# Feed-forward expert sum as one chain of adds on GpSimd, gated products written in place into an eight-slot ring

## Chip, cores and metric

One core of a Trainium2 chip runs the whole program. The metric is the device time of one execution in microseconds (us). Five engines work at the same time and wait for each other through semaphores: TensorE (PE in the profile), VectorE (DVE), ScalarE (ACT), GpSimd (POOL), and SyncE (SP), which issues the transfers.

## What is computed

The reference is a layer of three parts on 4 x 512 tokens of width 256: half a mixture-of-experts feed-forward, attention, and the same half feed-forward again with the same weights. The change touches only the feed-forward, which runs twice:

```python
def _L0_ffn_ref(x, router_w, router_b, expert_w, expert_b, proj_w, proj_b, norm_w):
    B, S, D = x.shape                      # 4, 512, 256
    E = router_b.shape[0]                  # 8
    logits = jnp.einsum('bsd,de->bse', x, router_w) + router_b
    topk_vals, topk_idx = jax.lax.top_k(logits, TOP_K)     # 2
    topk_w = jax.nn.softmax(topk_vals, axis=-1)
    full_w = jnp.sum(jax.nn.one_hot(topk_idx, E, dtype=x.dtype) * topk_w[..., None], axis=-2)
    h = jnp.einsum('td,edf->etf', xf, expert_w) + expert_b[:, None, :]
    expert_out = jax.nn.silu(h)
    combined = jnp.einsum('etf,te->tf', expert_out, full_w.reshape(-1, E)).reshape(B, S, D)
    out = jnp.einsum('bsd,df->bsf', combined, proj_w) + proj_b
    y = x + out
    rms = jnp.sqrt(jnp.mean(y * y, axis=-1, keepdims=True) + EPS)
    return norm_w * (y / rms)
...
x = x + 0.5 * _L0_ffn_ref(_layernorm(x, axis=-1), ...)
```

All eight experts are computed for every token; a token's weight is zero for six of them. `combined` is the sum that the change rebuilds.

## The kernel before

`ffn_phase` is called twice, first with the prefix f1 (the first some 170 us of the span) and then with f2 (the last some 150 us); attention lies between. Each phase takes the tokens in four batches of 512 (`SEQ`). Batch 0 is written out, batches 1 and 2 are a hardware loop (`Fori(1, LAST)`), batch 3 is written out with `more=False`. Every engine has its own program, in which `body(i, prev, more)` is batch `i`; nothing is scheduled by a planner, and the order on an engine is the order in which its code is written. The profile drops the prefix and the buffer number, so that f_s is `s_ring` of either phase.

Within a batch the features lie on the 128 partitions in two halves (`C = 2`, index `f`) and the tokens along the free axis, so that one tile is 128x512 in float32. For each expert `e` and half `f`, with `n = 2e + f`:

- TensorE forms the expert's product in bank `ex_ps[n % 4]` with six matmuls (L749 to L751), and spreads the token's weight for expert `e` over the partitions with one matmul into `w_ps[e % 2]` (`select`, L762).
- ScalarE applies silu into `s_ring[n % 4]` (L603). It waits for `mult_done`, so that the slot's previous product has been read.
- VectorE multiplies the slot by the weight in `w_ps` (L482). The product of expert 0 goes to `acc`, the others to `u_ring[n % 4]`.
- The sum: GpSimd adds the products of experts 1, 2 and 3 to `acc` (L293). VectorE adds product 4 to product 5, and 6 to 7, as pairs in `u_ring` (L506, two instructions of 128x512 a pair), and GpSimd adds each pair to `acc` by two more L293. That makes 10 adds on GpSimd and 4 on VectorE a batch. Between expert 3 and the pairs, GpSimd's program has `residual` (L256, z plus the projection's bias) and `add_rows` (L275, the previous batch's result added to x; not in batch 0).

What follows the sum of batch `i` runs inside batch `i + 1`. ScalarE rounds `acc` to `ch` (`sum_lead`, L610), VectorE takes the remainder `cl` (`sum_rest`, L403), TensorE projects them into `w_ps` (`project`, L771 to L773, 24 matmuls), VectorE adds the residual (L436), ScalarE squares (L620), VectorE forms the mean square (L441), GpSimd its inverse root (`inverse_rms`, L270), and VectorE scales the rows (`scale_rows`, L446). `acc` is free for batch `i + 1` once `cl` is there.

VectorE's `gating` of batch `i + 1` (L364 to L393) comes right after the last product and pair of batch `i`, and before `sum_rest(i)`. It is a chain of some twenty small instructions that ends in `fw`. TensorE transposes `fw` (`weights_T`, L735) and then runs `project(i)`; both stand in its program behind experts 0, 1 and 2 of batch `i + 1`. The inputs of some of these small instructions all lie in SBUF (the gap of the two best logits L372, the cast of the indices L376, the one-hot rows and what is made of them L379 to L393); the first two (L364, L367) have one input in PSUM, as L482 has.

In phase f1 alone, ScalarE and VectorE also split the attention weights into two parts (L628, L452; 128x1280), and GpSimd scales them (L265).

Batch 3 sums otherwise: GpSimd adds products 1 and 2 to `acc`, then forms 3 + 4 + 5 in place (L303, L308), and VectorE forms 6 + 7 and adds both (L409, L416).

Of the kernel before, what the change touches and what calls it, by code (L numbers as in the profile page):

```python
# [15 lines left out]
F32 = mybir.dt.float32  # L16
# [40 lines left out]
def ffn_phase(nc, tag, d, shared, step_sems, passed, first, split, out):  # L57
# [16 lines left out]
    with ExitStack() as ctx:  # L74
# [41 lines left out]
        fw = sb("fw", [P, BT, P])  # L116
        wT = sb("wT", [P, SEQ], F32R)

        s_ring = [sb(f"s{n}", [P, SEQ]) for n in range(4)]
        u_ring = [sb(f"u{n}", [P, SEQ]) for n in range(4)]  # L120
        acc = sb("acc", [P, C, SEQ])
        ch, cl = sb("ch", [P, C, SEQ], F32R), sb("cl", [P, C, SEQ], F32R)

# [1 line left out]
        pick_raw = sq[0:2 * E].rearrange("p t d -> p (t d)").rearrange("p (e q) -> p e q", e=E)  # L125


        last5 = sq[:].rearrange("p (c t) d -> p c (t d)", c=C)
        ch_last, cl_last = e_hi[:, 0:C, :], e_lo[:, 0:C, :]
        ss, ms, rr = sb("ss", [P, BT]), sb("ms", [P, BT]), sb("rr", [P, BT])  # L130
        if first:
# [25 lines left out]
        step_ps = t_ps + w_ps + w_ps  # L157
        RING = len(ex_ps)
        SILU0 = RING
        MULT0 = len(s_ring)  # L160
        X0 = 1


        SUMS = (1, 2, 3, 5, 7)
        ACC = C * len(SUMS)
        PAIRS = C * 2
        GATE = 20
        LAST = BATCH - 1

# [71 lines left out]
        def _(pool):  # L241
# [35 lines left out]
            def body(i, prev, more):  # L277
                if more or first:
                    rstd(i + 1)
                if prev:  # L280
                    inverse_rms(i - 1)
                if first:
                    scale_queries(i)
                for j, e in enumerate(SUMS if more else SUMS[:2]):
                    for f in range(C):
                        n = C * e + f
                        if e < 4:
                            pool.wait_ge(mult_done, MULT0 + C * E * i + n + 1)
                        else:
                            pool.wait_ge(pair_done, PAIRS * i + C * (e // 2 - 2) + f + 1)  # L290
                        if j > 0:
                            pool.wait_ge(acc_done, ACC * i + C * (j - 1) + f + 1)
                        pool.tensor_tensor(acc[:, f, :], acc[:, f, :], u_ring[n % 4][:], ALU.add).then_inc(acc_done, 1)  # L293
                    if e == 3:
                        residual(i + 1)
                        if prev:
                            add_rows(i - 1)
                if not more:

                    for f in range(C):  # L300
                        e3, e4 = (u_ring[(C * e + f) % 4] for e in (3, 4))
                        pool.wait_ge(mult_done, MULT0 + C * E * i + C * 4 + f + 1)
                        pool.tensor_tensor(e4[:], e4[:], e3[:], ALU.add).then_inc(acc_done, 1)  # L303
                    for f in range(C):
                        e4 = u_ring[(C * 4 + f) % 4]
                        pool.wait_ge(mult_done, MULT0 + C * E * i + C * 5 + f + 1)
                        pool.wait_ge(acc_done, ACC * i + C * 2 + f + 1)
                        pool.tensor_tensor(e4[:], e4[:], last5[:, f, :], ALU.add).then_inc(acc_done, 1)  # L308
                    add_rows(i - 1)

            if first:
# [12 lines left out]

        @block.vector
        def _(dve):
            dve.sem_inc(mult_done, MULT0)

            def norm_stats(j):
                b, k = block_of(j), (j - J0) * BT  # L330
                if isinstance(j, int) and j >= BATCH:
# [72 lines left out]

            def add_sixth(f):

                e6, e7 = s_ring[(C * 6 + f) % 4], s_ring[(C * 7 + f) % 4]
                dve.wait_ge(mult_done, MULT0 + C * E * LAST + C * 7 + f + 1)
                dve.tensor_tensor(e7[:], e7[:], e6[:], ALU.add).then_inc(pair_done, 1)  # L409

            def add_middle(f):

                e7 = s_ring[(C * 7 + f) % 4]
                dve.wait_ge(pair_done, PAIRS * LAST + 2 * f + 1)
                dve.wait_ge(acc_done, ACC * LAST + C * 3 + f + 1)
                dve.tensor_tensor(e7[:], e7[:], u_ring[(C * 4 + f) % 4][:], ALU.add).then_inc(pair_done, 1)  # L416

            def last_rest():
                for f in range(C):
                    dve.wait_ge(chi_done, C * BATCH + f + 1)  # L420
                    dve.tensor_tensor(cl_last[:, f, :], s_ring[(C * 7 + f) % 4][:], ch_last[:, f, :].bitcast(F32),
                                      ALU.subtract).then_inc(clo_done, 1)

            def add_last_residual(t):
# [29 lines left out]
            def body(i, prev, more):  # L454
                if not prev:
                    norm_stats(i + 1)
                gating(i)
                if prev:
                    sum_rest(i - 1)
                    if more or first:  # L460
                        norm_stats(i + 1)
                    add_residual(i - 1, 0)
                    add_residual(i - 1, 1)
                else:
                    norm_rows(i + 1)
                    expert_rest(4)
                    expert_rest(5)
                group_at = (3, 6) if more else (2, 3)
                for e in range(E):
                    for f in range(C):  # L470
                        n = C * e + f
                        dve.wait_ge(silu_done, SILU0 + C * E * i + n + 1)
                        if f == 0:
                            dve.wait_ge(sel_done, E * i + e + 1)
                        if e in (3, 4) or more and e in (5, 7):
                            dve.wait_ge(acc_done, ACC * i + C * (3 if e == 7 else e - 3) + f + 1)
                        if more and e == 6:
                            dve.wait_ge(pair_done, PAIRS * i + f + 1)
                        to = acc[:, f, :] if e == 0 else u_ring[n % 4][:]
                        if not more and e >= 5:  # L480
                            to = last5[:, f, :] if e == 5 else s_ring[n % 4][:]
                        dve.tensor_tensor(to, s_ring[n % 4][:], w_ps[e % 2][:], ALU.mult).then_inc(mult_done, 1)  # L482
                        if not more and e == E - 1:
                            if f > 0:
                                add_middle(f - 1)
                            add_sixth(f)
                    if e == 0 and prev:
                        mean_square(i - 1)
                    if e == 0 and prev and (more or first):
                        norm_rows(i + 1)  # L490
                    if e == 0 and not prev:
                        expert_rest(6)
                        expert_rest(7)
                        dve.wait_ge(e_hi_done, E + 1)
                        dve.tensor_tensor(p_lo[:], p_raw, p_hi[:].bitcast(F32), ALU.subtract).then_inc(p_split, 1)
                    if e == 2 and prev:
                        scale_rows(i - 1)
                    if e == 4 and (more or first):
                        z_rest(i + 1)
                    if e == 4 and not more:  # L500
                        sum_rest(i)
                    if more and e in (5, 7):
                        dve.wait_ge(mult_done, MULT0 + C * E * i + C * e + C)
                        for f in range(C):
                            even, odd = u_ring[(C * (e - 1) + f) % 4], u_ring[(C * e + f) % 4]
                            dve.tensor_tensor(odd[:], odd[:], even[:], ALU.add).then_inc(pair_done, 1)  # L506
                    if first and e in group_at:
                        group_rest(i, group_at.index(e))
                if not more:
                    add_middle(C - 1)  # L510
# [62 lines left out]
        def _(act):  # L573
# [24 lines left out]
            def silu(i, e, chunks=range(C)):  # L598
                for f in chunks:
                    n = C * e + f  # L600
                    act.wait_ge(ex_done, C * E * i + n + 1)
                    act.wait_ge(mult_done, C * E * i + n + 1)
                    act.activation(s_ring[n % 4][:], ex_ps[n % RING][:], ACT.Silu,  # L603
                                   bias=e_bias[:, n:n + 1]).then_inc(silu_done, 1)

            def sum_lead(i):
# [4 lines left out]

            def last_lead():
                for f in range(C):
                    act.wait_ge(pair_done, PAIRS * LAST + 2 * f + 2)
                    act.activation(ch_last[:, f, :], s_ring[(C * 7 + f) % 4][:], ACT.Copy).then_inc(chi_done, 1)

            def squares(i):
                for t in range(BT):
# [79 lines left out]
        def _(pe):  # L698
# [55 lines left out]
            def select(i, e, prev):  # L754
# [3 lines left out]
                if e < 2 and prev:  # L758
                    pe.wait_ge(yadd_done, 2 * (i - 1) + e + 1)
                if e >= 2:  # L760
                    pe.wait_ge(mult_done, MULT0 + C * E * i + C * (e - 1))
                pe.matmul(w_ps[e % 2][:], pick[:, e, :], wT[:], start=True, stop=True).then_inc(sel_done, 1)  # L762

            def project(i):
# [34 lines left out]
            def step_project(k):  # L799

                if k == 2:
                    pe.wait_ge(mult_done, MULT0 + C * E * BATCH)
# [837 lines left out]
```

## Time and profile before

| | us |
|---|---|
| median of three runs | 892.91 (891.31 to 893.33) |
| the profiled execution | 892.65 |
| its span, from the first to the last instruction | 890.8 |
| busy: PE, DVE, POOL, ACT | 822.6, 701.0, 585.2, 521.4 |
| mean granted TensorE clock | 0.971 of full |

The span is a little shorter than the time of the same execution; what lies around it is 1.85 us. The busy times are over the whole span, and attention, which the change doesn't touch, takes some 570 us of it. A matmul's busy time overlaps with the next one's, so that PE's share reads higher than its work.

### The profile page before, as it was taken

To read this page: it belongs to the slowest core of one execution; us is meant where nothing else is said; L and a number is where in the kernel's file an instruction comes from. 1 tells how busy PE (TensorE), PEld (TensorE's weight loads), DVE (VectorE), ACT (ScalarE), POOL (GpSimd) and SP (SyncE) were. 2 spreads that over 40 slices of the span, in tenths; PEclk is the share of its full clock that TensorE was granted. 3 is DMA by queue.
4 is the path that set the end of the run, shared out by engine and by line. 5 is a ranking of instruction groups with operands and counts; after the bars stand their busy time and mean duration, and the time that the engine had idled before them with its cause. 6 is when DMAs were issued, how large, how long until landed. Compare 5 with 4: busy or idle time off the path is not lost. (4 is left out here: it accounts for less than half of the span.)

```text
span 890.8 us, 17017 instructions
## 1 busy us (share of the span) xinstructions
PE 822.6 (92%) x4848; PEld 724.0 (81%) x4848; DVE 701.0 (79%) x1824; ACT 521.4 (59%) x1252; POOL 585.2 (66%) x444
## 2 busy tenths in 40 slices
PE   5998888767999999999999999999999998999984
PEld 4776776656889999999999899899999986787873
DVE  6899989899776776776866867767767797789987
ACT  3654534445765765755865766756767663554542
POOL 3667746368587687777777787777777812556743
PEclk9999988978999999999999999999999999899998
DMA  8053153410212311312312312212212100000001
GB/s 302 1 178 105 72 201 142 142 36 12 49 24 59 106 24 35 94 35 59 94 24 47 94 24 71 85 33 47 71 41 54 25 1 29 1 1 24 24 1 47
DMA packets 26673, 55.98 MB, mean 63 GB/s; under 512 B 3568, under 2 KB 9840, under 8 KB 25104
## 3 DMA queue, kind: packets, MB, share of 16 engines
q1 hardware_dynamic: 26640, 55.59, 21.4%
q8 instruction: 15, 0.25, 0.1%
q14 instruction: 18, 0.15, 0.1%
HBM read 22.02 MB, written 12.58 MB: 39 GB/s over the span
## 5 line engine op out<-in xcount | busy, mean ns | idle before, releaser
L1050 POOL TENSOR_TENSOR at_ql<-at_rot,at_qh 128x512 fp32r<-128x512 f32 x62 | 79.8, 1287 | 99.6 <-ACT at_qh L1272 99.6
L1289 ACT ACTIVATE at_pr<-at_sm,at_low 128x512 f32<-128x512 f32 (+3 forms) x256 | 140.4, 555 | 0.9 <-DVE at_low L1137 0.8
L1295 ACT ACTIVATE at_pth<-at_pt 128x512 fp32r<-128x512 f32 (+1 forms) x192 | 95.8, 525 | 76.0 <-PE at_pt L1449 75.2
L603 ACT ACTIVATE f_s<-f_ex,f_cols 128x512 f32<-128x512 f32 x128 | 84.1, 686 | 86.0 <-PE f_ex L751 46.3
L293 POOL TENSOR_TENSOR f_acc<-f_acc,f_u 128x512 f32<-128x512 f32 x68 | 100.8, 1509 | 40.8 <-DVE f_u L482 27.7
L1147 DVE TENSOR_SCALAR at_pr<-at_pr,at_inv 128x128 f32<-128x128 f32 (+3 forms) x256 | 113.1, 504 | 2.3
L1137 DVE CUSTOM_DVE_ANT_0 at_sm<-at_sc,at_mask 128x512 f32<-128x512 f32 (+3 forms) x256 | 109.8, 484 | 2.5 <-issue 2.4
L1152 DVE TENSOR_TENSOR at_ptl<-at_pt,at_pth 128x512 fp32r<-128x512 f32 (+1 forms) x192 | 108.7, 593 | 1.7 <-ACT at_pth L1295 1.5
L1059 POOL TENSOR_TENSOR at_rot<-ga,cos 128x512 f32<-128x512 f32 x78 | 104.2, 1336 | 4.1 <-POOL at_ql L1050 2.4
L1065 POOL TENSOR_TENSOR at_rot<-at_rot,gc 128x512 f32<-128x512 f32 x78 | 101.5, 1301 | 8.1 <-POOLq L1082 2.1
L1449 PE MATMUL at_pt<-ident,at_pr 128*128 128x128 f32 x640 | 96.3, 278 | 9.3 <-DVE at_pr L1147 6.8
L1061 POOL TENSOR_TENSOR gc<-gc,sin 128x512 f32<-128x512 f32 x78 | 102.2, 1311 | 0.0
L749 PE MATMUL f_ex<-zh,f_e_hi 128*128 128x512 f32 (+1 forms) x240 | 97.5, 406 | 0.0
L750 PE MATMUL f_ex<-zl,f_e_hi 128*128 128x512 f32 (+1 forms) x240 | 96.8, 403 | 0.0
L751 PE MATMUL f_ex<-zh,f_e_lo 128*128 128x512 f32 (+1 forms) x240 | 96.3, 401 | 0.0
L1272 ACT ACTIVATE at_qh<-at_rot 128x512 fp32r<-128x512 f32 x64 | 40.4, 631 | 92.8 <-POOL at_rot L1065 90.7
L1436 PE MATMUL at_sc<-at_kh,at_qh 128*128 (+4 forms) x256 | 89.4, 349 | 3.9 <-DVE at_ql L1228 3.9
L1449 PEld LDWEIGHTS at_pt<-ident,at_pr 128*128 128x128 f32 x640 | 73.2, 142 | 15.4 <-DVE at_pr L1147 7.6
L1437 PE MATMUL at_sc<-at_kl,at_qh 128*128 (+4 forms) x256 | 84.1, 328 | 0.0
L1438 PE MATMUL at_sc<-at_kh,at_ql 128*128 (+4 forms) x256 | 83.7, 327 | 0.0
L1463 PE MATMUL at_o<-at_pth,at_vh 128*128 128x512 f32 (+3 forms) x256 | 82.7, 323 | 0.0
L1465 PE MATMUL at_o<-at_pth,at_vl 128*128 128x512 f32 (+3 forms) x256 | 82.5, 322 | 0.0
(212 smaller groups left out, 2262.7 us busy)
## 6 DMA issues: line engine op xcount, KB each, us to landing
gc<-ga SPq DMA_DIRECT2D x160, 128.0 KB, 2.3
ga<-in_attn_w SPq DMA_DIRECT2D x4, 1280.0 KB, 7.7
attn_split<-gb SPq DMA_DIRECT2D x4, 1280.0 KB, 9.6
attn_split<-gc SPq DMA_DIRECT2D x4, 1280.0 KB, 12.1
gb<-attn_split SPq DMA_DIRECT2D x8, 512.0 KB, 4.2
at_wo<-attn_split SPq DMA_DIRECT2D x8, 512.0 KB, 4.3
x<-in_x SPq DMA_DIRECT2D x4, 512.0 KB, 9.0
e_raw<-in_expert_w SPq DMA_DIRECT2D x8, 256.0 KB, 6.7
```

Source lines behind the costliest of these rows:

```text
L293: pool.tensor_tensor(acc[:, f, :], acc[:, f, :], u_ring[n % 4][:], ALU.add).then_inc(acc_done, 1)
L749: pe.matmul(bank, hi[:, w], zh[:, c, b], start=(c == 0), stop=False)
L750: pe.matmul(bank, hi[:, w], zl[:, c, b], start=False, stop=False)
L751: r = pe.matmul(bank, lo[:, w], zh[:, c, b], start=False, stop=(c == C - 1))
L1059: pool.tensor_tensor(rot[r % 2][:], raw[r], cosT[:], ALU.mult)
L1061: pool.tensor_tensor(swap[r], swap[r], sinT[:], ALU.mult).then_inc(sin_done, 1)
L1065: pool.tensor_tensor(rot[r % 2][:], rot[r % 2][:], swap[r], ALU.add).then_inc(sum_done, 1)
L1137: dve.tensor_tensor_reduce(out=sm[h % 2][:, OFF[i]:OFF[i] + w], in0=sc[bank][:, col:col + w], in1=mask[:, SEQ - w:SEQ], scale=1.0, scalar= ...
L1147: dve.tensor_scalar(a, a, inv[h % 2][:, i:i + 1], None, ALU.mult).then_inc(nm_done, 1)
L1152: dve.tensor_tensor(ptl[h % 2][:, cols], pt[(NF * h + k) % 2][:, 0:FLEN[k]], pth[h % 2][:, cols].bitcast(F32), ALU.subtract).then_inc(lo_d ...
L1289: act.activation(pr[h % 2][:, cols], sm[h % 2][:, cols], ACT.Exp, bias=low[h % 2][:, i:i + 1], scale=-1.0, accum_out=tot[h % 2][:, i:i + 1 ...
L1449: r = pe.transpose(pt[(NF * h + k) % 2][:, col + (i - kt) * P:col + (i - kt + 1) * P], pr[h % 2][:, OFF[i] + kt * P:OFF[i] + (kt + 1) * P] ...
```

## The change

The pair adds on VectorE are gone. GpSimd adds the products of experts 1 to 7 to `acc` one after the other, 14 adds a batch in batches 0 to 2. `u_ring` is gone, and `s_ring` has eight slots in its place: VectorE writes the product over the silu that it was made from, and GpSimd reads it there. So a slot is free for the silu four experts later only when GpSimd has added it (for expert 4, when VectorE has made product 0, which goes to `acc` and leaves the slot unused). In batch 3 the places of some products change, the number of adds and their engines don't.

```diff
-        s_ring = [sb(f"s{n}", [P, SEQ]) for n in range(4)]
-        u_ring = [sb(f"u{n}", [P, SEQ]) for n in range(4)]
+        s_ring = [sb(f"s{n}", [P, SEQ]) for n in range(8)]
...
-        SUMS = (1, 2, 3, 5, 7)
+        SUMS = range(1, E)
...
                 for j, e in enumerate(SUMS if more else SUMS[:2]):
                     for f in range(C):
                         n = C * e + f
-                        if e < 4:
-                            pool.wait_ge(mult_done, MULT0 + C * E * i + n + 1)
-                        else:
-                            pool.wait_ge(pair_done, PAIRS * i + C * (e // 2 - 2) + f + 1)
+                        pool.wait_ge(mult_done, C * E * i + n + 1)
                         if j > 0:
                             pool.wait_ge(acc_done, ACC * i + C * (j - 1) + f + 1)
-                        pool.tensor_tensor(acc[:, f, :], acc[:, f, :], u_ring[n % 4][:], ALU.add).then_inc(acc_done, 1)
+                        pool.tensor_tensor(acc[:, f, :], acc[:, f, :], s_ring[n % SLOTS][:], ALU.add).then_inc(acc_done, 1)
                     if e == 3:
                         residual(i + 1)
                         if prev:
...
                         dve.wait_ge(silu_done, SILU0 + C * E * i + n + 1)
                         if f == 0:
                             dve.wait_ge(sel_done, E * i + e + 1)
-                        if e in (3, 4) or more and e in (5, 7):
-                            dve.wait_ge(acc_done, ACC * i + C * (3 if e == 7 else e - 3) + f + 1)
-                        if more and e == 6:
-                            dve.wait_ge(pair_done, PAIRS * i + f + 1)
-                        to = acc[:, f, :] if e == 0 else u_ring[n % 4][:]
-                        if not more and e >= 5:
-                            to = last5[:, f, :] if e == 5 else s_ring[n % 4][:]
-                        dve.tensor_tensor(to, s_ring[n % 4][:], w_ps[e % 2][:], ALU.mult).then_inc(mult_done, 1)
+                        slot = s_ring[n % SLOTS][:]
+                        to = acc[:, f, :] if e == 0 else slot
+                        dve.tensor_tensor(to, slot, w_ps[e % 2][:], ALU.mult).then_inc(mult_done, 1)
...
-                    if more and e in (5, 7):
-                        dve.wait_ge(mult_done, MULT0 + C * E * i + C * e + C)
-                        for f in range(C):
-                            even, odd = u_ring[(C * (e - 1) + f) % 4], u_ring[(C * e + f) % 4]
-                            dve.tensor_tensor(odd[:], odd[:], even[:], ALU.add).then_inc(pair_done, 1)
...
                     act.wait_ge(ex_done, C * E * i + n + 1)
-                    act.wait_ge(mult_done, C * E * i + n + 1)
-                    act.activation(s_ring[n % 4][:], ex_ps[n % RING][:], ACT.Silu,
+                    if e == 4:
+                        act.wait_ge(mult_done, C * E * i + f + 1)
+                    elif e > 4:
+                        act.wait_ge(acc_done, ACC * i + C * (e - 5) + f + 1)
+                    elif not (isinstance(i, int) and i == 0):
+                        act.wait_ge(acc_done, ACC * (i - 1) + C * (e + 3) + f + 1)
+                    act.activation(s_ring[n % SLOTS][:], ex_ps[n % RING][:], ACT.Silu,
                                    bias=e_bias[:, n:n + 1]).then_inc(silu_done, 1)
```

GpSimd's program at the end of batch 0 of phase f1, from the residual on; before:

```order
L256 TENSOR_TENSOR f1_zres<-z,f1_rows 128x1024
L293 TENSOR_TENSOR f1_acc<-f1_acc,f1_u2 128x512
L293 TENSOR_TENSOR f1_acc<-f1_acc,f1_u3 128x512
L293 TENSOR_TENSOR f1_acc<-f1_acc,f1_u2 128x512
L293 TENSOR_TENSOR f1_acc<-f1_acc,f1_u3 128x512
```

The same place now (the changed kernel's lines are numbered anew, L287 is the add to `acc`):

```order
L253 TENSOR_TENSOR f1_zres<-z,f1_rows 128x1024
L287 TENSOR_TENSOR f1_acc<-f1_acc,f1_s0 128x512
L287 TENSOR_TENSOR f1_acc<-f1_acc,f1_s1 128x512
L287 TENSOR_TENSOR f1_acc<-f1_acc,f1_s2 128x512
L287 TENSOR_TENSOR f1_acc<-f1_acc,f1_s3 128x512
L287 TENSOR_TENSOR f1_acc<-f1_acc,f1_s4 128x512
L287 TENSOR_TENSOR f1_acc<-f1_acc,f1_s5 128x512
L287 TENSOR_TENSOR f1_acc<-f1_acc,f1_s6 128x512
L287 TENSOR_TENSOR f1_acc<-f1_acc,f1_s7 128x512
```

Four adds behind the residual have become eight; in batches 1 and 2 `add_rows` stands between the residual and them, before and now.

VectorE's program at the same place, from the products of expert 5 to the cast in the gating; before:

```order
L482 TENSOR_TENSOR f1_u2<-f1_s2,f1_wide1 128x512
L482 TENSOR_TENSOR f1_u3<-f1_s3,f1_wide1 128x512
L506 TENSOR_TENSOR f1_u2<-f1_u2,f1_u0 128x512
L506 TENSOR_TENSOR f1_u3<-f1_u3,f1_u1 128x512
L482 TENSOR_TENSOR f1_u0<-f1_s0,f1_wide0 128x512
L482 TENSOR_TENSOR f1_u1<-f1_s1,f1_wide0 128x512
L452 TENSOR_TENSOR gc<-ga,gb 128x1280
L482 TENSOR_TENSOR f1_u2<-f1_s2,f1_wide1 128x512
L482 TENSOR_TENSOR f1_u3<-f1_s3,f1_wide1 128x512
L506 TENSOR_TENSOR f1_u2<-f1_u2,f1_u0 128x512
L506 TENSOR_TENSOR f1_u3<-f1_u3,f1_u1 128x512
```

And now (L469 is the product, L444 the split of the attention weights):

```order
L469 TENSOR_TENSOR f1_s2<-f1_s2,f1_wide1 128x512
L469 TENSOR_TENSOR f1_s3<-f1_s3,f1_wide1 128x512
L469 TENSOR_TENSOR f1_s4<-f1_s4,f1_wide0 128x512
L469 TENSOR_TENSOR f1_s5<-f1_s5,f1_wide0 128x512
L444 TENSOR_TENSOR gc<-ga,gb 128x1280
L469 TENSOR_TENSOR f1_s6<-f1_s6,f1_wide1 128x512
L469 TENSOR_TENSOR f1_s7<-f1_s7,f1_wide1 128x512
```

The four pair adds have left VectorE, and what followed each pair stands right behind the products; the gating is next in both.

## Rows read from the trace of the kernel before

**Rows 1.** Busy time by stretch: stretch, us, busy (instructions) by engine, granted clock, DMA.

```profile
50.00:80.00 30.00, 26.52 (x126) 21.59 (x125) 29.05 (x53) 15.57 (x29) 21.11 (x15) 0.94 0.24 97
...
819.00:851.00 32.00, 29.76 (x148) 24.64 (x148) 30.26 (x72) 15.68 (x31) 21.22 (x14) 1.00 0.05 17
```

**Rows 2.** Timeline of TensorE, ends of batches: start, us, what [idle before, releaser].

```profile
52.08 0.66 PE L735 MATMUL f_t<-ident,f_fw 128*128 128x128 f32 x4 [0.33 <-DVE f_fw L393]
...
87.79 0.66 PE L735 MATMUL f_t<-ident,f_fw 128*128 128x128 f32 x4 [1.15 <-DVE f_fw L393]
...
123.34 1.11 PE L735 MATMUL f_t<-ident,f_fw 128*128 128x128 f32 x4 [2.55 <-DVE f_fw L393]
...
787.50 0.60 PE L735 MATMUL f_t<-ident,f_fw 128*128 128x128 f32 x4
...
819.09 0.66 PE L735 MATMUL f_t<-ident,f_fw 128*128 128x128 f32 x4 [1.60 <-DVE f_fw L393]
820.29 0.39 PE L771 MATMUL f_wide<-f_p_hi,f_ch 128*128 128x256 f32 x1 [0.55 <-DVE f_cl L403]
```

**Rows 3.** Timeline of GpSimd, phase f2, batch 1.

```profile
795.47 5.41 POOL L293 TENSOR_TENSOR f_acc<-f_acc,f_u 128x512 f32<-128x512 f32 x4 [0.65 <-DVE f_u L482]
...
807.19 2.84 POOL L275 TENSOR_TENSOR x<-x,f_y 128x1024 f32 x1
810.00 3.00 POOL L293 TENSOR_TENSOR f_acc<-f_acc,f_u 128x512 f32<-128x512 f32 x2
814.60 2.83 POOL L293 TENSOR_TENSOR f_acc<-f_acc,f_u 128x512 f32<-128x512 f32 x2 [1.61 <-DVE f_u L506]
```

**Rows 4.** Timeline of VectorE, phase f2, batch 1 and the gating behind it.

```profile
797.10 4.45 DVE L446 SCALAR_TENSOR_TENSOR f_y<-f_y,f_rr,f_rows 128x256 f32<-128x256 f32 x4
...
806.37 4.21 DVE L506 TENSOR_TENSOR f_u<-f_u 128x512 f32<-128x512 f32 x2
...
814.96 0.18 DVE L364 TENSOR_TENSOR f_l<-f_t,f_rows 128x32 f32<-128x32 f32 x1
...
815.93 0.28 DVE L372 TENSOR_TENSOR f_gap<-f_top 128x4 f32<-128x4 f32 x1
...
816.81 0.66 DVE L376 CAST f_topf<-f_topi 128x8 f32<-128x8 uint32 x1
...
818.09 0.18 DVE L386 TENSOR_TENSOR f_oh<-f_oh,f_w 128x32 f32<-128x32 f32 x1
```

**Rows 5.** Timeline of GpSimd, phase f1, batches 0 and 1.

```profile
38.59 2.42 POOL L256 TENSOR_TENSOR f_zres<-z,f_rows 128x1024 f32<-128x1024 f32 x1
...
47.51 2.92 POOL L293 TENSOR_TENSOR f_acc<-f_acc,f_u 128x512 f32<-128x512 f32 x2 [1.60 <-DVE f_u L506]
...
74.40 2.39 POOL L275 TENSOR_TENSOR x<-x,f_y 128x1024 f32 x1
...
83.30 2.84 POOL L293 TENSOR_TENSOR f_acc<-f_acc,f_u 128x512 f32<-128x512 f32 x2 [1.60 <-DVE f_u L506]
```

**Rows 6.** Timeline of VectorE, phase f1, the second split in batch 1.

```profile
79.06 1.48 DVE L452 TENSOR_TENSOR gc<-ga,gb 128x1280 fp32r<-128x1280 f32 x1
```

**Rows 7.** The adds on GpSimd by their line: count, ns min/median/max.

```profile
L293 POOL TENSOR_TENSOR f_acc<-f_acc,f_u x68: 1263/1315/2637, 29.8 to 863.3; 128x512 f32<-128x512 f32 x68
```

**Rows 8.** Timeline of GpSimd and VectorE, phase f2, batch 0.

```profile
765.71 7.56 POOL L293 TENSOR_TENSOR f_acc<-f_acc,f_u 128x512 f32<-128x512 f32 x6 [10.92 <-DVE f_u L482]
...
781.61 2.92 POOL L293 TENSOR_TENSOR f_acc<-f_acc,f_u 128x512 f32<-128x512 f32 x2 [1.60 <-DVE f_u L506]
...
785.78 0.17 DVE L382 TENSOR_SCALAR f_w<-f_th 128x4 f32<-128x4 f32 x1 [0.89 <-ACT f_th L587]
```

**Rows 9.** Busy time by stretch: the 24 matmuls of a projection, twice.

```profile
88.90:91.80 2.90, 2.81 (x24) 2.81 (x25) 2.59 (x11) 0.20 (x2) 0.74 (x1) 1.00 0.98 413
124.50:129.80 5.30, 5.25 (x24) 5.25 (x25) 2.55 (x10) 1.50 (x5) 1.02 (x1) 0.50 1.00 409
```

**Rows 10.** Timeline of VectorE, phase f1, batch 3.

```profile
150.50 1.87 DVE L482 TENSOR_TENSOR f_s<-f_s,f_wide 128x512 f32<-128x512 f32 x3
```

More of the change, by code:

```diff
@@ L125, in ffn_phase @@
         pick_raw = sq[0:2 * E].rearrange("p t d -> p (t d)").rearrange("p (e q) -> p e q", e=E)
-        last5 = sq[:].rearrange("p (c t) d -> p c (t d)", c=C)
         ch_last, cl_last = e_hi[:, 0:C, :], e_lo[:, 0:C, :]
@@ L159, in ffn_phase @@
         SILU0 = RING
-        MULT0 = len(s_ring)
+        SLOTS = len(s_ring)
         X0 = 1
-        SUMS = (1, 2, 3, 5, 7)
+        SUMS = range(1, E)
         ACC = C * len(SUMS)
-        PAIRS = C * 2
         GATE = 20
@@ L300, in body @@
                     for f in range(C):
-                        e3, e4 = (u_ring[(C * e + f) % 4] for e in (3, 4))
-                        pool.wait_ge(mult_done, MULT0 + C * E * i + C * 4 + f + 1)
+                        e3, e4 = (s_ring[(C * e + f) % SLOTS] for e in (3, 4))
+                        pool.wait_ge(mult_done, C * E * i + C * 4 + f + 1)
                         pool.tensor_tensor(e4[:], e4[:], e3[:], ALU.add).then_inc(acc_done, 1)
                     for f in range(C):
-                        e4 = u_ring[(C * 4 + f) % 4]
-                        pool.wait_ge(mult_done, MULT0 + C * E * i + C * 5 + f + 1)
+                        e4, e5 = (s_ring[(C * e + f) % SLOTS] for e in (4, 5))
+                        pool.wait_ge(mult_done, C * E * i + C * 5 + f + 1)
                         pool.wait_ge(acc_done, ACC * i + C * 2 + f + 1)
-                        pool.tensor_tensor(e4[:], e4[:], last5[:, f, :], ALU.add).then_inc(acc_done, 1)
+                        pool.tensor_tensor(e4[:], e4[:], e5[:], ALU.add).then_inc(acc_done, 1)
                     add_rows(i - 1)
@@ L326, in _ @@
         def _(dve):
-            dve.sem_inc(mult_done, MULT0)
             def norm_stats(j):
@@ L405, in add_sixth @@
             def add_sixth(f):
-                e6, e7 = s_ring[(C * 6 + f) % 4], s_ring[(C * 7 + f) % 4]
-                dve.wait_ge(mult_done, MULT0 + C * E * LAST + C * 7 + f + 1)
+                e6, e7 = (s_ring[(C * e + f) % SLOTS] for e in (6, 7))
+                dve.wait_ge(mult_done, C * E * LAST + C * 7 + f + 1)
                 dve.tensor_tensor(e7[:], e7[:], e6[:], ALU.add).then_inc(pair_done, 1)
             def add_middle(f):
-                e7 = s_ring[(C * 7 + f) % 4]
-                dve.wait_ge(pair_done, PAIRS * LAST + 2 * f + 1)
+                e4, e7 = (s_ring[(C * e + f) % SLOTS] for e in (4, 7))
+                dve.wait_ge(pair_done, 2 * f + 1)
                 dve.wait_ge(acc_done, ACC * LAST + C * 3 + f + 1)
-                dve.tensor_tensor(e7[:], e7[:], u_ring[(C * 4 + f) % 4][:], ALU.add).then_inc(pair_done, 1)
+                dve.tensor_tensor(e7[:], e7[:], e4[:], ALU.add).then_inc(pair_done, 1)
             def last_rest():
@@ L420, in last_rest @@
                     dve.wait_ge(chi_done, C * BATCH + f + 1)
-                    dve.tensor_tensor(cl_last[:, f, :], s_ring[(C * 7 + f) % 4][:], ch_last[:, f, :].bitcast(F32),
+                    dve.tensor_tensor(cl_last[:, f, :], s_ring[(C * 7 + f) % SLOTS][:], ch_last[:, f, :].bitcast(F32),
                                       ALU.subtract).then_inc(clo_done, 1)
@@ L613, in last_lead @@
                 for f in range(C):
-                    act.wait_ge(pair_done, PAIRS * LAST + 2 * f + 2)
-                    act.activation(ch_last[:, f, :], s_ring[(C * 7 + f) % 4][:], ACT.Copy).then_inc(chi_done, 1)
+                    act.wait_ge(pair_done, 2 * f + 2)
+                    act.activation(ch_last[:, f, :], s_ring[(C * 7 + f) % SLOTS][:], ACT.Copy).then_inc(chi_done, 1)
             def squares(i):
@@ L760, in select @@
                 if e >= 2:
-                    pe.wait_ge(mult_done, MULT0 + C * E * i + C * (e - 1))
+                    pe.wait_ge(mult_done, C * E * i + C * (e - 1))
                 pe.matmul(w_ps[e % 2][:], pick[:, e, :], wT[:], start=True, stop=True).then_inc(sel_done, 1)
@@ L801, in step_project @@
                 if k == 2:
-                    pe.wait_ge(mult_done, MULT0 + C * E * BATCH)
+                    pe.wait_ge(mult_done, C * E * BATCH)
                 if k >= 4:
```

## Prediction

> **What bounds the kernel now.** I read the page first, then the busy time by stretch, then TensorE's timeline at the ends of the batches, and last GpSimd's and VectorE's beside each other. The page's totals mix three phases, so the stretches matter more: VectorE is busy for 29.05 of 30 us in the loop of f1 and 30.26 of 32 in that of f2, TensorE for 26.5 and 29.8, GpSimd for 21.1 and 21.2 [rows 1]. That reads like a case for taking work from VectorE. But a share doesn't say who ends last. TensorE waits at one place in each batch of both phases: before `weights_T`, for `fw`, and once more, by 0.55 us, before `project`, for `cl` [rows 2]. In f2 it starts `weights_T` at 819.09 after 1.60 idle and `project` at 820.29. So what a batch costs is set by when the gating chain and the last add to `acc` are done, and GpSimd has a hand in both. The last add of f2's batch 1 ends at 814.60 + 2.83 = 817.43 [rows 3]; the gating's cast, begun at 816.81, takes 0.66 and ends with it [rows 4], while the same chain's other small instructions take 0.2 to 0.3. It stands still while GpSimd adds.
>
> The second thing to see is how the two engines alternate. `scale_rows` is four instructions of 256 columns with both inputs in SBUF. Beside four adds on GpSimd they take 4.45 us together, 1.1 each [rows 4], and the adds 5.41, 1.35 each [rows 3]: one of VectorE, one of GpSimd, in turn. With nothing in SBUF against them, six adds take 7.56, 1.26 each [rows 8], and none of the 68 took under 1.263 [rows 7].
>
> **The change, part by part.** *GpSimd's tail.* After `add_rows` (in batch 0 after `residual`) there are now eight adds in place of four. Everything up to there depends on `project` of the batch before and not on the pairs, so it starts where it did. In f2's batch 1 `add_rows` starts at 807.19. It took 2.84 beside VectorE's pair, 2.39 without one in f1 [rows 3, 5], and the pair is gone: the adds start at 809.6. By then the products are there: the rest of VectorE's list before the gating is six products, free of the 4.21 us that the pair took [rows 4]. I count three adds at 1.26 until the gating asks for its first SBUF pair, and five at 1.35 in turn with it: 10.5 us, the end at 820.1 in place of 817.43, **2.7 later**. The bounds are 8 x 1.26 = 10.1 and 8 x 1.35 = 10.8, that is 2.3 to 3.0. In f1's batch 1, `add_rows` ends at 74.40 + 2.39 = 76.8 [rows 5], and the second split (1.48 [rows 6]) gets its turn among the adds: 76.8 + 10.5 + 1.5 = 88.8 in place of 83.30 + 2.84 = 86.14, **2.7 later**; batch 2 is the same. In f1's batch 0 the residual ends at 38.59 + 2.42 = 41.0, and the adds at 53.0 in place of 50.43 [rows 5], **2.6 later**. In f2's batch 0 the residual ends at 765.71 + 7.56 + 2.42 = 775.7 [rows 5, 8], the adds at 786.2 in place of 784.53 [rows 8], **1.7 later**.
>
> *The gating.* VectorE reaches it earlier, by the pairs; in f2 it then waits for TensorE's logits, in f1 it can start some 1.3 us sooner. That helps nothing if it must take turns: from the gap on, at least eight of its instructions have all inputs in SBUF (the gap, the cast, two one-hot rows, two weightings, their sum, the remainder in `fw`), while five or fewer adds are left. Each add lets one of them through, so the chain ends only behind the last add, with what is then left of it. Before, the chain from the second weighting (818.09) to TensorE's start (819.09) took 1.0 [rows 2, 4]; I take 1.0 + 0.1 behind the last add. `weights_T` would start at 821.2 in f2 (+2.1), 89.9 in f1's batch 1 (from 87.79, +2.1), 125.5 in its batch 2 (from 123.34, +2.1), 54.1 in its batch 0 (from 52.08, +2.0). `project` keeps its 1.2 us behind it. In f2's batch 0 the gating waits for ScalarE's tanh at 785.78 already [rows 8], and `weights_T` had no wait at 787.50 [rows 2]; I take +0.6. Bounds for each place: +1.2, if the chain slips through between adds (then only `cl` waits for the last add: 2.7 less the 1.5 by which `project` at 820.29 trails the last add beyond the two 0.6 us steps of `ch` and `cl`), and +3.0. Six places: 2.0 + 2.1 + 2.1 + 0.6 + 2.1 + 2.1 = **11.0 us**.
>
> On this row and rule differ in what they count. The Trainium skill, page "SBUF — State Buffer", section "Who interferes with whom", has the lock on the shared ports as exclusive for the whole instruction, and lists scalar-operand instructions, copies and casts among those that can take it. By that page the two weights L382 and L383 would wait for a turn too, an estimate of 0.3 us more at each of five places, 1.5 in all. The same page says that issue order decides who blocks; it doesn't say that the two alternate, which [rows 3, 4] show.
>
> *TensorE's clock.* In f1 its wait of 1.15 us before `weights_T` of batch 1 was followed by a projection at granted clock 1.00 in 2.90 us, the wait of 2.55 in batch 2 by one at 0.50 in 5.30 us [rows 2, 9]. So a halved clock costs 2.4 there, at once, since GpSimd's whole list hangs on the projection. The waits become 1.15 + 2.1 = 3.3, 1.60 + 2.1 = 3.7 in f2 twice, and 0.33 + 2.0 = 2.3 in f1's batch 0; f1's batch 2 pays already, and f2's batch 0 has no such wait. Three places for certain enough, one at even chance: 2.4 x 3.5 = **8.4 us**. Bounds: none, or 2.4 at four places, 9.6.
>
> *Costed at nothing.* The pair adds leave VectorE (4 a batch, 4.21 for the costlier two of f2 [rows 4]): TensorE is what waits, and it waits behind GpSimd. If that cover were gone, this would be the gain of the rival below. The product in place: same inputs, one in PSUM, same length. The new waits of silu on `acc_done`: behind silu of expert 4 to 7 stand adds of experts 1 to 3, done long before; behind those of the next batch's experts 0 and 1 stand the adds of 4 and 5, of which the last ends at about 83.3 in f1 and 815 in f2, level with TensorE's own product. What queues behind a late one is the tanh on ScalarE and then the two weights, which wait for GpSimd's turn anyway; priced from 0 to 0.3. Batch 3: its silu of expert 7 is released sooner, but VectorE runs expert 6 and 7 in one piece from 150.50 for 1.87 [rows 10], so nothing comes of it.
>
> **Sum.** 11.0 + 8.4 = 19.4 on the profiled execution's own 892.65 (span 890.8) gives 912.0. That execution is within 0.3 of the median of the runs, 892.91, so the prediction is **912 us**, 2.1% slower.
>
> **Rivals.**
>
> 1. *GpSimd is late, but the gating slips through.* If VectorE gets more than one small instruction done between two adds, `weights_T` starts nearly on time and only `project` waits: 5 x 1.2 + 0.3 = 6.3, and TensorE's wait is cut in two, so that the clock halves at perhaps one place more: 899 to 903, say 901. For it: the small instructions take under 0.2. Against it: `scale_rows`, four in a row without a dependence, took strict turns.
>
> 2. *Faster.* VectorE is what ends last, and losing the pairs lets the gating start sooner. TensorE's waits of 0.33, 1.15 and 2.55 in f1 and 1.60 twice in f2 could go [rows 2], at most 7.2 with the 0.55 left, and with one halved clock (2.4) 9.6: 883 to 887. It decides at the length of an add: the eight must end by 817.43 from 809.6, so each within 0.98 us. None of the 68 was under 1.263 [rows 7]. Only if the gating held the ports first and the adds weren't what `cl` waits for could this win.
>
> 3. *No change.* The lateness is hidden behind the 1.5 us of slack at `cl`, and the gating's earlier start pays for its turns: 893. It needs adds that end at most 1.5 later; I work out 2.7, at least 2.3.
>
> 4. *Slower still.* The halved clock reaches into the expert products behind the projection and into silu's waits, 1.5 to 2 more at each of five places: 920 to 923.
>
> **How the numbers follow.** The main case has 0.62, with its own range 905 to 918 (places at +1.6 to +2.6, two to four halved clocks). Rival 1 has 0.18, rival 2 0.07, rival 3 0.05, rival 4 0.08. A measurement of this kernel can tell some 0.2%, 1.8 us, from no change. Slower is 0.62 + 0.18 + 0.08 = 0.88, same 0.05, faster 0.07. The range leaves out rivals 2, 3, 4 and reaches into rival 1 to 899; at the top 919.
>
> **What the changed profile would show.** Eight adds in a row on GpSimd behind `add_rows`, 10 to 11 us in f2 and 12 in f1, with GpSimd idle only before `rstd`; the gap, cast and one-hot instructions of the gating at 1.2 to 1.4 us apart in place of 0.2; `weights_T` 3.3 to 3.7 us idle for `fw`; granted clock 0.5 in most projections; VectorE's busy time down by about 20 us and its waits up; a loop period of f2 of some 36 us in place of 32. It would be wrong if the chain of the gating ends before GpSimd's last add (rival 1), if the projections keep clock 1.00 after waits over 3 us (8 us less), or if adds run shorter than 1.26.

## The result, and the profile after

The changed kernel takes 904.24 us (median of four, 903.23 to 906.58) against 892.11 in the runs beside it: ratio 1.0146, interval 1.0129 to 1.0163, slower by some 12 us. Each experiment below has its ratio to runs of the kernel before made beside it, whose medians lie between 891.33 and 891.79; a difference between two other kernels is that of their medians, and is good to about 1 us. The profiled executions have spans of 901.4 and 890.8, so the profile has 10.6 of it.

TensorE's timeline at the ends of the batches, changed kernel, against [rows 2]:

```profile
53.27 0.66 PE L722 MATMUL f_t<-ident,f_fw 128*128 128x128 f32 x4 [1.81 <-DVE f_fw L385]
...
91.72 1.12 PE L722 MATMUL f_t<-ident,f_fw 128*128 128x128 f32 x4 [2.45 <-DVE f_fw L385]
...
129.70 1.12 PE L722 MATMUL f_t<-ident,f_fw 128*128 128x128 f32 x4 [3.92 <-DVE f_fw L385]
...
825.39 1.08 PE L722 MATMUL f_t<-ident,f_fw 128*128 128x128 f32 x4 [3.20 <-DVE f_fw L385]
```

The waits of 0.33, 1.15, 2.55 and 1.60 us are now 1.81, 2.45, 3.92 and 3.20, and the fifth, behind f2's batch 2, is 3.28 in place of 1.65. GpSimd's timeline, phase f2, batch 1, against [rows 3]:

```profile
809.55 2.41 POOL L253 TENSOR_TENSOR f_zres<-z,f_rows 128x1024 f32 x1
811.91 2.40 POOL L272 TENSOR_TENSOR x<-x,f_y 128x1024 f32 x1
814.26 9.97 POOL L287 TENSOR_TENSOR f_acc<-f_acc,f_s 128x512 f32<-128x512 f32 x8
```

Eight adds run without a hole, 1.25 us each, right behind `add_rows`. VectorE's gating beside them, against [rows 4]:

```profile
816.76 0.19 DVE L356 TENSOR_TENSOR f_l<-f_t,f_rows 128x32 f32<-128x32 f32 x1 [2.80 <-PE f_t L716]
...
817.74 0.33 DVE L364 TENSOR_TENSOR f_gap<-f_top 128x4 f32<-128x4 f32 x1
818.66 0.66 DVE L368 CAST f_topf<-f_topi 128x8 f32<-128x8 uint32 x1
819.36 1.24 DVE L371 TENSOR_TENSOR f_oh<-f_rows,f_topf 128x32 f32<-128x32 f32 x1
820.51 1.32 DVE L372 TENSOR_TENSOR f_oh<-f_rows,f_topf 128x32 f32<-128x32 f32 x1
821.76 1.28 DVE L374 TENSOR_SCALAR f_w<-f_th 128x4 f32<-128x4 f32 x1
822.96 1.30 DVE L375 TENSOR_SCALAR f_w<-f_th 128x4 f32<-128x4 f32 x1
824.29 0.19 DVE L377 TENSOR_TENSOR f_oh<-f_oh,f_w 128x32 f32<-128x32 f32 x1
...
825.16 0.18 DVE L385 TENSOR_TENSOR f_fw<-f_full,f_full_hi 128x32 f32<-128x32 f32 x1
825.26 1.28 DVE L395 TENSOR_TENSOR f_cl<-f_acc,f_ch 128x512 fp32r<-128x512 f32 x2
```

Four instructions of 32 or 4 columns (L371 to L375) take 1.24 to 1.32: one for each add. In the kernel before, where the last add ended at 817.43, the same ones took 0.2 and less:

```profile
817.50 0.19 DVE L379 TENSOR_TENSOR f_oh<-f_rows,f_topf 128x32 f32<-128x32 f32 x1
...
817.72 0.16 DVE L382 TENSOR_SCALAR f_w<-f_th 128x4 f32<-128x4 f32 x1
```

The last add ends at 824.23, and the next instruction (L377) is back at 0.19. VectorE waited 2.80 us for TensorE's logits before all this: its head start was worth nothing there.

The projections' stretches in the changed kernel (stretch, us, busy by engine, granted clock), to be read with [rows 9]; each ends with its last residual add:

```profile
54.47:59.00 4.53, 4.53 (x26) 4.49 (x27) 2.51 (x10) 0.70 (x4) 1.02 (x1) 0.67 0.29 122
92.90:97.20 4.30, 4.28 (x26) 4.24 (x27) 2.61 (x11) 1.24 (x4) 1.02 (x1) 0.75 0.05 19
130.90:136.30 5.40, 5.40 (x25) 5.39 (x26) 2.50 (x11) 1.46 (x5) 1.02 (x1) 0.53 0.36 133
793.10:796.30 3.20, 3.20 (x26) 3.16 (x27) 2.54 (x11) 0.57 (x4) 1.02 (x1) 1.00 0.00 0
826.60:830.80 4.20, 4.20 (x26) 4.16 (x27) 2.50 (x10) 1.02 (x4) 1.02 (x1) 0.73 0.00 0
861.20:866.60 5.40, 5.40 (x25) 5.40 (x26) 0.69 (x1) 1.42 (x5) 0.00 (x0) 0.52 0.00 0
```

Five of the six meet a halved clock for part or all of their time (a mean between 0.5 and 1 is a stretch that is part at 1.2 and part at 2.4 GHz). Only the one after f2's batch 0, with no wait ahead of `weights_T`, is at 1.00. The length of the wait alone doesn't say how much of a projection is halved: behind 3.20 us it took 4.22, behind 3.28 it took 5.48, and in the kernel before 3.16 behind 1.60 us.

### The profile page after: what moved, and what is told of

Its sections match the earlier page's. It is cut to its first block and busy times, and to the rows that moved or that the text cites. A ratio compares the mean times of both kernels' runs of the same rounds, so it can differ in the third digit from the quotient of the medians.

```text
span 901.4 us, 16986 instructions
## 1 busy us (share of the span) xinstructions
PE 828.0 (92%) x4848; PEld 729.1 (81%) x4848; DVE 698.5 (77%) x1800; ACT 521.6 (58%) x1252; POOL 609.4 (68%) x468
## 3 DMA queue, kind: packets, MB, share of 16 engines
q1 hardware_dynamic: 26640, 55.59, 21.2%
## 5 line engine op out<-in xcount | busy, mean ns | idle before, releaser
L287 POOL TENSOR_TENSOR f_acc<-f_acc,f_s 128x512 f32<-128x512 f32 x92 | 125.8, 1400 | 26.2 <-DVE f_s L469 26.2
```

The source lines that it names most:

```text
L287: pool.tensor_tensor(acc[:, f, :], acc[:, f, :], s_ring[n % SLOTS][:], ALU.add).then_inc(acc_done, 1)
```

## Where the 10.6 us of the profile are

I cut each phase at two events, the start of `project` and the last residual add behind it, in both traces; batch 0 of each phase counts from the phase's first `weights_T`.

| part | f1 b0 | f1 b1 | f1 b2 | f2 b0 | f2 b1 | f2 b2 | sum |
|---|---|---|---|---|---|---|---|
| up to `project`: adds and gating | 1.50 | 1.43 | 1.39 | -1.35 | 1.59 | 1.56 | 6.1 |
| the projection: clock | 1.31 | 1.03 | -0.08 | 0.00 | 1.06 | 2.44 | 5.8 |

For f2's batch 1, for example, the last residual add before it starts at 791.53 and `project` at 820.29 before (28.76), 796.25 and 826.60 after (30.35). The rest, -1.3, is 0.3 ahead of the first `weights_T`, 0.2 in attention (neither traced) and 0.8 behind the last projection. That last one is a loss of 0.4 in batch 3, where VectorE now waits 1.57 us for the silu of expert 7, and a gain of 1.2 in the last 11 us, where the granted clock is 0.69 before and 0.80 after. The -1.35 is by the clock too: it lies behind f2's wait for the first `fw` (3.1 us in both kernels); there the granted clock of the next 8 us is 0.57 before and 0.78 after:

```profile
757.10:765.00 7.90, 7.11 (x20) 5.51 (x21) 5.51 (x12) 3.44 (x6) 0.00 (x0) 0.57 0.00 0
```

```profile
763.20:771.00 7.80, 7.02 (x26) 5.60 (x27) 6.92 (x14) 4.69 (x8) 0.73 (x1) 0.78 0.00 0
```

Adds and gating cost 7.5 us at five places. The other 3 are mostly clock: 5.8 lost in the projections, 1.35 and 1.2 gained elsewhere.

## The experiments

**The ring alone.** The change has two parts. This run has the eight slots and the product in place, and the pairs back on VectorE:

```diff
-        SUMS = range(1, E)
+        PAIRED = (5, 7)
+        SUMS = [e for e in range(1, E) if e + 1 not in PAIRED]
...
+                    if more and e in PAIRED:
+                        dve.wait_ge(mult_done, C * E * i + C * e + C)
+                        for f in range(C):
+                            even, odd = s_ring[(C * (e - 1) + f) % SLOTS], s_ring[(C * e + f) % SLOTS]
+                            dve.tensor_tensor(odd[:], odd[:], even[:], ALU.add).then_inc(pair_done, 1)
```

> The eight-slot ring and the product in place alone; the pair adds stay on VectorE (10 adds a batch on GpSimd, 4 on VectorE, as before). Theory (the cost is GpSimd's chain of eight adds behind add_rows, and the gating taking turns with it): 892 us, within 2 of before, adds ending where they did. Rival (silu now waits for GpSimd's adds through the ring, and that costs): 898 to 904, with ScalarE waiting for acc.

886.27 us, ratio 0.9926 (0.9906 to 0.9945). Neither was right: the ring costs nothing, and it gains 6. Taken in this order, the ring first and the chain on top of it, the change is a gain of 6 and a loss of some 18 in one. VectorE's products of experts 6 and 7, f2, batch 1, in this run:

```profile
806.69 2.47 DVE L474 TENSOR_TENSOR f_s<-f_s,f_wide 128x512 f32<-128x512 f32 x4
809.20 1.29 DVE L498 TENSOR_TENSOR f_s<-f_s 128x512 f32<-128x512 f32 x2
```

Four products in one piece, the pair right behind. In the kernel before, the last product of expert 7 waited for GpSimd to have added the pair that lay in its slot.

**The ring with VectorE's old waits for GpSimd put back,** those of experts 3, 4, 5 and 7. In the kernel before, as in this run, VectorE stood idle for one of them only, once a batch, for 3.5 us in all.

```diff
+                        if e in (3, 4) or more and e in (5, 7):
+                            dve.wait_ge(acc_done, ACC * i + C * (3 if e == 7 else e - 3) + f + 1)
                         slot = s_ring[n % SLOTS][:]
```

> The ring with the pairs kept (886.3), and VectorE's old waits for acc_done ahead of the products of experts 3, 4, 5 and 7 put back; nothing else. Theory (the ring's 6 us come from the product of expert 7 no longer waiting 0.6 us for GpSimd at each batch's end): the wait of 0.5 to 0.7 is back in each of six batches, the last adds end where they did before: 890 to 893. Rival (they come from silu no longer waiting for the product four earlier): 886.

891.98 us, ratio 0.9999 (0.9988 to 1.0011). The 6 us are gone, all of them, and the rival with them:

```profile
808.83 1.95 DVE L476 TENSOR_TENSOR f_s<-f_s,f_wide 128x512 f32<-128x512 f32 x3
811.34 0.69 DVE L476 TENSOR_TENSOR f_s<-f_s,f_wide 128x512 f32<-128x512 f32 x1 [0.56 <-POOL f_acc L292]
812.92 2.85 POOL L292 TENSOR_TENSOR f_acc<-f_acc,f_s 128x512 f32<-128x512 f32 x2 [1.61 <-DVE f_s L500]
```

The wait totals 3.5 us in six places. From `project` to the last add of f2's batch 1 it is 29.10 us here and 28.33 without it. The other 2 to 3 us are not traced one by one; TensorE's waits before `weights_T` are shorter in the ring alone (0.87 in f2's batch 1, 1.61 here), with fewer halved clocks behind them (mean clock 0.976 and 0.969).

**Half the chain.** Only the pair 6 + 7 on VectorE (`PAIRED = (7,)`), 12 adds on GpSimd.

> The changed kernel with the pair 6 + 7 back on VectorE: 12 adds a batch on GpSimd, 2 on VectorE. Theory: the tail behind add_rows is six adds in place of eight, 2.5 us shorter, and about two of the gating's turns go with it; at each of five places between 0 and 0.8 us late in place of 1.2 to 1.6, hardly a halved clock: 893 to 898, say 895. Rival (only that VectorE's pairs are gone matters, by VectorE reaching the gating early): half way, 898.

892.49 us, ratio 1.0006 (0.9987 to 1.0024), just under the range expected. Two adds more on GpSimd than the ring alone cost 6, four cost 18. Six adds behind `add_rows` take 8.42 us, with the pair among them.

**The gating without its turns.** The cast, the weights, the weighted row and the sum go into free columns of the logits' PSUM bank, so that nearly every instruction of the chain has at most one input in SBUF. GpSimd's program is untouched. Done to the changed kernel and to the kernel before:

```diff
                 lp = t_ps[1][:].rearrange("p (t k) -> p t k", t=BT)
+                topf, half0, full = lp[:, :, 16:18], lp[:, :, 24:32], lp[:, :, 40:48]
+                w0, w1 = lp[:, :, 48:49], lp[:, :, 49:50]
...
-                dve.tensor_tensor(oh0[:], oh0[:], w0[:].unsqueeze(2).to_broadcast([P, BT, E]), ALU.mult).then_inc(gate, 1)
+                dve.tensor_tensor(half0, oh0[:], w0.to_broadcast([P, BT, E]), ALU.mult).then_inc(gate, 1)
```

> The changed kernel with the gating's small tiles (index, weights, weighted row, sum) in free columns of the PSUM bank of the logits, so that of its instructions only the gap and the copy into fw have all operands in SBUF. GpSimd's adds stay as they are. Theory (the gating is late because its instructions take turns with the adds): cast, one-hot rows and weights at under 0.3 us each in place of 1.2 to 1.3, weights_T without a wait for fw in f2, project 1.4 us behind the last add in place of 2.4, some waits now short enough to keep the clock: 895 to 899, say 897. Rival (only the last add's end matters, the gating's delay is hidden): 904.

> The kernel before with the gating's small tiles in PSUM. Theory (the turns cost the kernel before too, at the cast): project 2.3 behind the last add in place of 2.85 at five places, so 0.5 each, and one more if a halved clock goes: 887 to 890, say 889. Rival: no change.

Changed kernel 898.97 us, ratio to before 1.0079 (1.0061 to 1.0097), 5 less than without the edit. Kernel before 887.79, ratio 0.9949 (0.9931 to 0.9968): the turns cost it too, and `project` follows the last add of f2's batch 1 by 2.34 us in place of 2.86. VectorE and TensorE of the first, f2, batch 1:

```profile
816.77 0.17 DVE L376 TENSOR_SCALAR f_t<-f_th 128x4 f32<-128x4 f32 x1 [1.21 <-ACT f_th L571]
...
818.16 0.18 DVE L387 TENSOR_TENSOR f_fw<-f_t,f_full_hi 128x32 f32<-128x32 f32 x1
...
818.40 0.65 PE L724 MATMUL f_t<-ident,f_fw 128*128 128x128 f32 x4
...
820.13 1.91 DVE L397 TENSOR_TENSOR f_cl<-f_acc,f_ch 128x512 fp32r<-128x512 f32 x2 [1.79 <-ACT f_ch L599]
...
822.10 0.58 PE L760 MATMUL f_wide<-f_p_hi,f_ch 128*128 128x256 f32 x1 [3.05 <-DVE f_cl L397]
```

`fw` is there in time, `weights_T` has no wait, and what is left is the last add itself: it ends at 820.66, `project` follows 1.44 behind it, in place of 2.37. The turns were 0.9 to 1.1 us at each of the five places. The lateness of the adds stays, and with it a wait of 3.05 us.

**The chain with a lighter list ahead of it.** `residual` goes from before the last eight adds to the head of the next batch's program, where GpSimd idles. Its work is the same.

```diff
                 if prev:
+                    residual(i)
                     inverse_rms(i - 1)
...
-                    if e == 3:
-                        residual(i + 1)
-                        if prev:
-                            add_rows(i - 1)
+                    if e == 3 and prev:
+                        add_rows(i - 1)
```

> The changed kernel with residual alone moved from before the last eight adds to the head of the next batch's program; the gating as it was. Theory (the chain costs by where it ends): the last add 2 us earlier at each of six places, project still 2.4 to 2.9 behind it by the turns, hardly a halved clock more than before: 890 to 894, say 892. Rival (GpSimd's total work, or the turns alone): 900 or more.

892.63 us, ratio 1.0006 (0.9991 to 1.0021): the 12 us are back, with 14 adds on GpSimd. Its timeline, f2, batch 1:

```profile
799.44 2.40 POOL L272 TENSOR_TENSOR x<-x,f_y 128x1024 f32 x1
801.80 10.03 POOL L288 TENSOR_TENSOR f_acc<-f_acc,f_s 128x512 f32<-128x512 f32 x8
```

The eight adds are as long as ever. They start 1.8 us sooner, counted from `project` (19.3 us in place of 21.2), and end 1.8 sooner (29.4 in place of 31.1); `weights_T` waits 1.48 in place of 3.20. So the greater part of the chain's cost, 12 of the 18 us over the ring alone, is its place behind a list that GpSimd could have worked off elsewhere. The other 6 stay.

One of the six places got worse by the edit. In batch 3 of f2 nothing holds `residual` back, and it runs right behind the last add. One instruction of the gating then waits for all of it:

```profile
843.67 2.37 POOL L253 TENSOR_TENSOR f_zres<-z,f_rows 128x1024 f32<-128x1024 f32 x1
```

```profile
843.71 2.35 DVE L373 TENSOR_SCALAR f_w<-f_th 128x4 f32<-128x4 f32 x1
```

`weights_T` waits 3.73 us there, and the projection behind it takes 5.24.

**Both edits together,** on the chain and on the ring with pairs, and the PSUM edit alone on the ring.

> The changed kernel (one chain of adds on GpSimd) with the gating's small tiles in PSUM and residual moved from before the last adds to the head of the next batch's program, where GpSimd waits. GpSimd's work is the same, 14 adds. Theory (the chain costs by standing last behind a full list, and not by the adds' own length): the adds end 2.4 us earlier at each of six places, project about level with TensorE's own work: 882 to 888, say 885, faster than before. Rival (GpSimd's total work binds the loop wherever it stands): no better than 896.

> The ring with the pairs kept, and the gating's small tiles in PSUM. Theory (here too the gating trails the last add only because it takes turns): project 1.4 us behind the last add in place of 2.85, but TensorE is nearly without a wait there already (0.3 to 1.9 us before weights_T), so it gains what is left of these waits: 880 to 884, say 882. Rival (no contention worth having with four adds): 886.

> The ring with the pairs kept on VectorE, the gating's small tiles in PSUM, and residual moved as above. Theory: no wait of TensorE before weights_T or project is left but for 0.5, TensorE bounds batches: 876 to 882, say 880; against the chain with the same two edits it is 2 to 6 faster. Rival (VectorE then ends last, and its pairs with it): slower than the chain with the same edits.

| kernel | us | ratio to before |
|---|---|---|
| chain, both edits | 889.70 | 0.9963 (0.9940 to 0.9986) |
| ring with pairs, PSUM | 883.71 | 0.9906 (0.9890 to 0.9922) |
| ring with pairs, both edits | 884.60 | 0.9899 (0.9869 to 0.9929) |

With both edits the chain beats the kernel before, by less than the 885 expected, and the pairs on VectorE stay ahead of it by 5. The trace has most of what is missing at the end of f2's batch 2, where `residual` again runs right behind the last add. The gating gets by now, but the remainder `cl` doesn't:

```profile
845.15 2.34 POOL L253 TENSOR_TENSOR f_zres<-z,f_rows 128x1024 f32<-128x1024 f32 x1
```

```profile
845.24 3.40 DVE L396 TENSOR_TENSOR f_cl<-f_acc,f_ch 128x512 fp32r<-128x512 f32 x2
```

The two instructions of `cl` take 1.28 us where GpSimd is idle. `project` starts 3.5 us behind the last add, against 1.44 with the PSUM edit alone, and takes 4.64 us against 3.16 at the full clock: some 3.6 us together. A `residual` held back there was not tried.

The ring with pairs and the gating in PSUM beats both kernels. Moving the residual on top of it gives nothing that can be told apart: TensorE has no wait left before `weights_T`, as expected, but the 2 us expected from that (882 and 880) didn't come. Its batches in f2 are shorter (30.0 and 30.4 us from `project` to `project` against 30.7 twice), and its stretch behind the last of them longer, 38.7 against 37.4, all of it in the last 12 and 10 us, where the granted clock is 0.70 against 0.84. Why the clock differs there was not tried.

**TensorE kept busy in its wait.** Eight matmuls of 512 columns ahead of `weights_T`, into the bank that it overwrites, in the changed kernel and in the kernel before.

```diff
+                if not (isinstance(j, int) and j == 0):
+                    for _ in range(8):
+                        pe.matmul(t_ps[0][:], r_hl[:, 0, :], zh[:, 0, 0:SEQ], start=True, stop=True)
                 pe.wait_ge(fw_done, j + 1)
```

> The changed kernel with eight 128x512 matmuls (1.8 us) in TensorE's wait before weights_T, in batches 1 to 3; their result is overwritten. Theory (some 4 of the 12 us are TensorE's halved clock after waits over 3 us): the waits left are under 2.2 us, the projections run at clock 1.00; 8 us back, 1.8 lost in f2 where there was no wait: 898, with granted clock 1.00 at all six projections. Rival (the halved clock costs nothing on the chain): 904 to 906.

> The kernel before with the same eight matmuls ahead of weights_T, as the ground for the one with them and the chain. Its waits there are 0.3 to 2.6 us, so the fill takes up to 1.5 at f1's batch 1 boundary and 1.8 in f2's first, and little elsewhere; it saves the halved clock of f1's batch 2 (2.4): 892 to 895, say 893. If the filled pair then differs by under 9, the difference to 12 is clock; if by 12, the clock was no part of it.

900.63 us, ratio 1.0092 (1.0060 to 1.0124), and 889.49, ratio 0.9971 (0.9956 to 0.9987). Work that nobody needs makes both kernels faster, by some 3.6 and 2.6 us, where the kernel before was expected at 892 to 895. It doesn't separate the clock's share of the change: in the filled kernel before, all six projections take 3.05 to 3.23 us, but in the filled changed one three still take 4.6 to 4.8 (all six were expected at the full clock), behind waits of 1.45 to 2.06 us that the fill leaves. The filled pair differs by 11, between the two bounds set for it.

## Why the prediction was right, and what it had wrong

It said slower, 912 us, by GpSimd's tail, the turns and the clock. Slower by that mechanism is what the runs show: the chain costs 18 over the ring alone, falls with the number of adds (6 for two), falls by 5 when the turns are taken away, and by 12 when the adds start 1.8 us sooner. The time is 8 us under the forecast, just below the main case's own 905 to 918, where rival 1's 899 to 903 ends; it is the traces that decide for the main case. The sum had the right terms, most of them too large (19.4 against 10.6 in the profile). In its order:

- *GpSimd's tail*: `add_rows` at 2.40 and the adds right behind it, as said; the adds start 18.0 us behind the last residual add, where 18.1 was forecast. "Five at 1.35 in turn" was wrong: eight took 9.97 us, 1.25 each, not 10.5. The 1.35 came from turns with `scale_rows`, 256 columns wide; small instructions cost the adds nothing. The split in f1 cost 1.3, not 1.5. The last add was 1.8 to 2.1 later at the five places, not 2.6 to 2.7.
- *The gating*: it took turns, and ended behind the last add at all five places where the two met closely. `weights_T` trails the last add by 1.16 in f2, against 1.1 assumed. The Trainium skill, page "SBUF — State Buffer", section "Who interferes with whom", has scalar-operand instructions among those that may take the shared ports; this trace agrees, L374 and L375 take 1.28 and 1.30. The 0.3 a place estimated by it doesn't show: the chain's end hangs on the last add, and turns taken before that cost it nothing. A place measured 1.4 to 1.6 in place of 2.0 to 2.1, and the five 7.5 in place of 10.4. f2's batch 0, forecast at 0.6 more, came out 1.35 shorter, by a clock that the forecast had no term for: luck.
- *The clock*: 5.8 in the projections, against 8.4. The forecast took a projection to be wholly halved or not at all. In three of the four that changed a part of it was: 4.2 to 4.5 us, with granted clock 0.67 to 0.75, for waits of 1.8, 2.45 and 3.2. Where else halved clocks fell gave back some 2.5 (1.35 and 1.2, above), which the forecast had no term for either.
- *Costed at nothing*: the product in place and the ring. The prediction went through silu's new waits, but not through the waits that the diff removes. Silu does wait for GpSimd's adds, in seven places, 5.7 us in all and 1.52 at most; no wait of TensorE or VectorE in the loop follows from it in the trace, but what it costs was not tried alone. Of the waits removed one, 0.6 us on the last product of each batch, is worth 6 us where the pairs follow it. It should be worth nothing in the changed kernel, where the adds are late anyway; no run has the chain with that wait. So slower was right although the forecast missed that one half of the change, by itself, is a gain.
- *The signs*: VectorE's busy time fell by 2.5 us, not by 20, since the turns count as busy. The batches of f2 take 33.5 and 34.6 us from `project` to `project`, not 36; only two of the six projections have a clock near 0.5; the gap of the logits and the cast took 0.33 to 1.23 and 0.66, not 1.2 to 1.4 each.

Of the rivals, the first (the gating slips through) is out: it didn't slip, and making it slip gave 899, near that rival's 899 to 903. "No change" needed adds that end at most 1.5 later, and they end 1.8 to 2.1 later. "Slower still" needed halved clocks beyond the projections to cost 1.5 to 2 more at each place; outside them the clock gave time back. The faster one named the price of an add under 0.98 us; the shortest of the 92 has a record of 1.252 (such records overlap a little, which is how eight fit in 9.97).

## What to carry to other kernels

Work moved to an engine with free time costs what stands behind it on the path: look where in that engine's program it lands and what waits for its last instruction, before counting the busy time of the other one. Small VectorE instructions with all operands in SBUF took turns with GpSimd's long ones here, one for one, so that the gating ended behind GpSimd's last add at all five places; with one operand or the result in PSUM it passed. What is moved on GpSimd to get it out of the way can itself land in front of such a chain, as `residual` did. When an edit replaces buffers, price the waits it removes as carefully as those it adds, and run the two halves of a change apart.

## What the runs showed of the hardware

- A VectorE instruction of 4 columns with a scalar operand, SBUF to SBUF, takes 1.3 us beside GpSimd's adds and 0.16 alone (one of 32 columns with two inputs: 1.24 to 1.32, and 0.19); with its result in PSUM it takes 0.17 beside them.
- The adds on GpSimd lose nothing to turns with instructions that small: 1.25 us each with four of them in between, 1.35 with instructions of 256 columns.
- Beside one GpSimd instruction of 128x1024, a VectorE instruction of 4 columns took 2.35 us.
- Eight needless matmuls in a wait gained 2.6 us in the kernel before (interval of the ratio 0.9956 to 0.9987).
